# A gated cross-attention and expert kernel on one core: the first batch's front re-ordered on all five queues

## What is computed

```python
x = x + tanh(g_xattn) * attention(layernorm(x), ctx, Wq, Wk, Wv, Wo)
#   scores = (q k^T) * 0.125 ; softmax over the 1601 keys ; out = att v ; concat Wo
x = x + tanh(g_ffn) * experts(layernorm(x))
#   router softmax over 8, top 2 renormalised; each expert gelu(x w1 + b1) w2 + b2
```

## Time and profile before

| | us |
|---|---|
| runs shown | 1294.05, 1299.71, 1299.17; median 1299.17 |
| the profiled execution's own time | 1296.63 |
| its span in the profile | 1294.8 |
| TensorE busy | 1248.2 (96%) |
| VectorE busy | 1123.0 (87%) |
| ScalarE busy | 1085.2 (84%) |
| GpSimd busy | 553.5 (43%) |

### The profile page before, as it was taken

The page is one execution under the profiler, slowest core; times in us unless marked ns, Lnnn a source line. Parts: engine busy times, 40 slices in busy tenths (PEclk is TensorE's granted clock), DMA queues, the critical chain, the costliest instruction groups (busy, mean ns, idle before and its releaser), DMA issues.

```text
span 1294.8 us, 42224 instructions
## 1 busy us (share of the span) xinstructions
PE 1248.2 (96%) x16259; PEld 629.0 (49%) x16259; DVE 1123.0 (87%) x2012; ACT 1085.2 (84%) x2196; POOL 553.5 (43%) x1213
## 2 busy tenths in 40 slices
PE   7999999999999999999999999999999999999992
PEld 2344444444444444444444444444444444499992
DVE  7889999999999999999999999999999999356434
ACT  2788998999898989999999998999999898866661
POOL 6324344353536262726252635445353512146551
PEclk9999999999999999999999999999999999999996
DMA  3332222212121212131212121222211110388896
GB/s 95 90 91 65 66 78 60 68 55 73 50 77 47 79 48 80 43 87 37 82 42 71 54 69 60 65 66 60 69 55 42 51 43 6 98 254 245 264 272 229
DMA packets 61092, 112.94 MB, mean 87 GB/s; under 512 B 13052, under 2 KB 36476, under 8 KB 60748
## 3 DMA queue, kind: packets, MB, share of 16 engines
q1 hardware_dynamic: 54187, 97.98, 25.8%
q0 software_dynamic: 4320, 8.99, 2.0%
q10 hardware_dynamic: 2385, 3.27, 0.7%
HBM read 52.77 MB, written 13.71 MB: 51 GB/s over the span
## 4 chain that ended last, share of the span: by engine, by line
PE 75%; SPq 9%; POOL 7%; DMA 3%; issue 2%; DVE 2%; ACT 1%; ACTq 0%; POOLq 0%; DVEq 0%
PE pv L912 28%; PE st L821 16%; PE mxp L875 12%; SPq L416 7%; PE st L798 6%; PE st L1130 5%; PE mxp L1140 5%; POOL kf L659 2%; DVE mx L1679 2%; POOL ksp L664 2%; POOL rows L723 1%; POOL ksp L662 1%; DMA qpack<-mxT 1%; POOL ksp L656 1%; DMA arena<-results 1%
## 5 line engine op out<-in xcount | busy, mean ns | idle before, releaser
L1679 DVE TENSOR_REDUCE mx<-mxp 128x2 f32<-128x1024 f32 x768 | 916.3, 1217 | 42.6 <-PE mxp L875 35.2
L1169 ACT ACTIVATE arena<-st 128x512 f32<-128x512 f32 (+1 forms) x1664 | 883.8, 597 | 66.8 <-PE st L821 53.1
L912 PE MATMUL pv<-arena 128*32 128x256 f32 x6656 | 531.6, 391 | 0.6 <-ACT pv_sb L1176 0.3
L821 PE MATMUL st<-qpack,kpack 51*128 51x256 bf16 (+1 forms) x3328 | 486.2, 272 | 4.9 <-DMA qpack<-mxT 4.6
L875 PE MATMUL mxp<-kpack,qpack 48*128 48x512 bf16 x1502 | 406.3, 382 | 1.3 <-DVE mx L1679 1.3
L821 PEld LDWEIGHTS st<-qpack,kpack 51*128 51x128 bf16 (+1 forms) x3328 | 195.1, 95 | 279.0 <-ACT arena L1169 149.6
L912 PEld LDWEIGHTS pv<-arena 128*32 128x32 f32 x6656 | 131.2, 108 | 173.8 <-issue 104.4
L690 POOL CAST mxs<-nmx 128x8 bf16<-128x8 f32 x64 | 12.2, 191 | 344.9 <-DVE nmx L1689 344.7
L875 PEld LDWEIGHTS mxp<-kpack,qpack 48*128 48x128 bf16 x1502 | 123.0, 93 | 67.2 <-issue 38.8
L1332 ACT ACTIVATE arena<-st,bias 128x256 f32<-128x256 f32 (+1 forms) x172 | 74.9, 437 | 45.5 <-PE st L1130 42.0
L723 POOL DMA_INDIRECT rows<-xrow,pos x64 | 65.9, 1030 | 89.9 <-DVE pos L1534 75.1
(11 more groups left out here) (202 smaller groups left out, 990.1 us busy)
## 6 DMA issues: line engine op xcount, KB each, us to landing
kpack<-ksp SPq DMA_DIRECT2D x756, 50.0 KB
arena<-in_w12T SPq DMA_DIRECT2D x43, 576.0 KB, 4.8
arena<-in_ctxT SPq DMA_DIRECT2D x15, 800.5 KB, 4.6
qpack<-qsp SPq DMA_DIRECT2D x187, 32.0 KB
xblk<-rows SPq DMA_DIRECT2D x28, 132.0 KB, 4.2
rows<-in_pads SPq DMA_DIRECT2D x8, 264.0 KB
arena<-results SPq DMA_DIRECT2D x8, 256.0 KB, 6.8
arena<-results ACTq DMA_DIRECT2D x8, 256.0 KB, 7.4
```

Of the source, the lines that this page charges most:

```text
L821: ins = eng.matmul(ring[i][0:n, jj * N:(jj + 1) * N], kpack[rows, b % 2, g * JJ + jj, kt * P:kt * P + n], qpack[rows, b % 2, g * JJ + jj, ...
L912: ins = eng.matmul(pv[32 * j:32 * j + 32, 0:N], vaug[0:n, b % 2, kt, at:at + 32], pt[0:n, (2 * u + rg) % PT_BUFS, jj * N:(jj + 1) * N], st ...
L1169: eng.activation(pt[0:n, c % PT_BUFS, :], ring[bank_of["S", u, p]][0:n, :], ACT.Exp, scale=SCALE).then_inc(s_exp, 1)
L1679: eng.tensor_reduce(mx[:, tj, w, :], src[:, :, 0:WIN], AX.X, ALU.max).then_inc(s_red, 1)
```

## The change

In batch 0's front and loop:

- the first root: ScalarE takes a square root of the variance, VectorE its reciprocal and one Newton step in place of an integer guess and three. An exponential of a dummy value follows on ScalarE;
- TensorE turns the rows after one chunk of keys and makes the queries after two; window 0 comes ahead of the fourth chunk. ScalarE's copies follow the same order;
- 20 windows run ahead of unit 0 in place of 18. The first 15 are fp32 windows, the last five use packs;
- all four chunks of batch 0's values come in the front, behind windows 14, 16, 17 and 18 (before: one chunk behind window 5, three in units 1, 6 and 7);
- batch 1's values come at units 0, 3, 7 and 15 (before: 25, 26, 27, 30), its keys at 5, 9, 14 and 18 (before: 8, 9, 10, 17);
- SP issues batch 1's context load and the two ones DMAs at the start; the high key packs of groups 0 and 1 go ahead of the low ones;
- in every batch, GpSimd waits for the earlier packs ahead of its first write to `ksp`, and ScalarE waits only for GpSimd's splits.

```diff
-FIRST_K_AT = {8: 0, 9: 1, 10: 2, 17: 3}
+FIRST_K_AT = {5: 0, 9: 1, 14: 2, 18: 3}
-FIRST, LEAD = 18, 23
+FIRST, LEAD = 20, 23
-FIRST_WINDOWS_AT = ("0100201010210011010100000110111100010011000111211000",
+FIRST_WINDOWS_AT = ("0100101010100111000200000011020100011011011101021010",
...
-EARLY = FIRST
+EARLY = NMX + 2
-FIRST_V, FIRST_TURN = 5, 14
-FIRST_V_AT, FIRST_X_AT, FIRST_Q_AT = {1: 1, 6: 2, 7: 3}, 3, 5
+FRONT_V, FIRST_TURN = {14: 1, 16: 1, 17: 1, 18: 1}, 14
+FIRST_V_AT, FIRST_X_AT, FIRST_Q_AT = {0: 4, 3: 5, 7: 6, 15: 7}, 0, 4
+FIRST_NEWTON = 1
...
@@ SP
-            eng.dma_start(id_sb[:, :], ident).then_inc(s_id, 16)
+            eng.dma_start(x_sb[:, NT:2 * NT, :], xs[:, 1, :, :]).then_inc(s_x1, 16)
+            eng.dma_start(wv_sb[:, :], wv).then_inc(s_wv, 16)
+            eng.dma_start(ctx_sb[:, 1, :], ctxT[1]).then_inc(s_ctx[1], 16)
...
-            first_keys_high(eng, 0)
+            eng.wait_ge(s_kone, 1)
+            ones_rows(0)
+            first_keys_high(eng, 0, 0)
             first_query_rows(eng, range(PARTS), 0)
             first_query_rows(eng, range(PARTS - 1, PARTS), 1)
-            first_keys_low(eng, 0)
-            other_keys(eng, 1, 0)
-            eng.wait_ge(s_kone, 1)
-            ones_rows(0)
+            first_keys_high(eng, 1, 0)
+            first_keys_low(eng, 0, 0)
+            first_keys_low(eng, 1, 0)
             eng.wait_ge(s_mxT, 1)
             place_half(eng, 0, 0)
             for rg in range(RG):
                 other_keys(eng, 2, rg)
-            eng.dma_start(ctx_sb[:, 1, :], ctxT[1]).then_inc(s_ctx[1], 16)
             pack_keys(0, 3)
...
@@ GpSimd, split_keys
                     eng.wait_ge(s_khi, NK * b + c + 1)
+                    if c == 0:
+                        for g in range(NG):
+                            eng.wait_ge(s_kd[(b - 1) % 2][g], 16 * PACKS * ((b - 1) // 2 + 1))
...
@@ ScalarE, first_keys
-                    if c == 0:
-                        for g in range(NG):
-                            eng.wait_ge(s_kd[(b - 1) % 2][g], 16 * PACKS * ((b - 1) // 2 + 1))
-                        if b == 1:
-                            eng.wait_ge(s_mxp, RG * EARLY)
+                    eng.wait_ge(s_k3, NK * (b - 1) + c + 1)
+                    if b == 1 and c == 0:
+                        eng.wait_ge(s_mxp, RG * EARLY)
...
@@ ScalarE, front
+            eng.wait_ge(s_var0, 1)
+            eng.activation(tmp[:, :], var[:, :], ACT.Sqrt).then_inc(s_root0, 1)
+            eng.wait_ge(s_id, 16)
+            eng.activation(warm[:, :], id_sb[:, 0:1], ACT.Exp)
             first_keys(0, 0)
+            copy_rows(0)
+            first_keys(0, 1)
             first_high(0)
...
@@ VectorE, front
+            for n in range(3):
+                norm_step("X", 0, n)
+            eng.wait_ge(s_root0, 1)
+            eng.reciprocal(rstd[:, :], tmp[:, :]).then_inc(s_seed, 1)
+            for n in range(4 * FIRST_NEWTON + 1):
+                first_norm(n)
```

More of the change, by code:

```diff
@@ L138, in windows, with front_values @@
     return [divmod(n, NMX) for n in range(issued(u, p), min(to, GROUPS * NMX))]
+def front_values(n):
+    done = sum(FRONT_V[k] for k in FRONT_V if k < n)
+    return range(done, done + FRONT_V[n])
 def rank_at(b):
@@ L154, in prepared @@
         return "K", b + 1, keys_at(b)[r]
-    if b + 1 < B and r in V_AT:
+    if 0 < b < B - 1 and r in V_AT:
         return "V", b + 1, V_AT[r]
@@ L170, in take @@
         taken += 1
-    take("V", 0, 0)
-    take("M", 0)
+    for n in range(FIRST):
+        if n in FRONT_V:
+            for c in front_values(n):
+                take("V", *divmod(c, NV))
+        if n == FIRST_TURN:
+            take("M", 0)
     for u in range(B * UNITS):
@@ L184, in ring_banks @@
         if b == 0 and r in FIRST_V_AT:
-            take("V", 0, FIRST_V_AT[r])
+            take("V", *divmod(FIRST_V_AT[r], NV))
         if u in (FIRST_X_AT, FIRST_Q_AT):
@@ L436, in first_keys_low @@
                 if K_KIND[part] > 0:
-                    pack_key_rows(eng, 0, 0, part, rg)
+                    pack_key_rows(eng, 0, g, part, rg)
         def first_query_rows(eng, parts, rg):
@@ L833, in early_window @@
                 pair, rows = G * NMX + m, slice(rg * RSTEP, (rg + 1) * RSTEP)
[L834 to L838, removed]
+                if pair < 2 and rg == 0:
+                    eng.wait_ge(s_qearly, pair + 1)
+                if pair == NMX and rg == 0:
+                    eng.wait_ge(s_qlater, EARLY_HEADS - JJ)
                 if pair == 1 and rg == 0:
@@ L900, in weighted @@
                     eng.wait_ge(s_khi, NK)
-                if b == 0 and g == 0:
-                    eng.wait_ge(s_v, next(c for c, (t0, tn) in enumerate(VCH) if kt < t0 + tn) + 1)
-                elif r == 0:
+                if r == 0:
                     eng.wait_ge(s_v, NV * (b + 1))
@@ L1049, in _ @@
             eng.wait_ge(s_wk, 16)
-            for c in range(NK - 2):
-                keys(0, c)
+            keys(0, 0)
             eng.wait_ge(s_id, 16)
             turn_rows("X", 0)
-            keys(0, NK - 2)
+            keys(0, 1)
             eng.wait_ge(s_wq, 16)
             queries(0)
-            keys(0, NK - 1)
-            for n in range(issued(0, 0)):
+            keys(0, 2)
+            for n in range(FIRST):
                 maximum(*divmod(n, NMX))
-                if n == FIRST_V:
+                if n == 0:
+                    keys(0, 3)
                     eng.wait_ge(s_wv, 16)
-                    values(0, 0)
-                elif n == FIRST_TURN:
+                if n in FRONT_V:
+                    for c in front_values(n):
+                        values(*divmod(c, NV))
+                if n == FIRST_TURN:
                     turn_maxima(0)
@@ L1079, in _ @@
                         keys(b + 1, keys_at(b)[r])
-                    elif r in V_AT:
+                    elif b > 0 and r in V_AT:
                         values(b + 1, V_AT[r])
                 if b == 0 and r in FIRST_V_AT:
-                    values(0, FIRST_V_AT[r])
+                    values(*divmod(FIRST_V_AT[r], NV))
                 if u == FIRST_X_AT:
@@ L1377, in norm_step @@
                     own += NT
+                elif n == 2 and norm_no[kind, b] == 0:
+                    eng.wait_ge(s_dve, own)
+                    eng.tensor_scalar(var[:, :], stat[:, :, 1], LN_EPS, None, ALU.add
+                                      ).then_inc(s_var0, 1)
                 elif n == 2:
@@ L1746, in _ @@
             own += 2
-            for n in range(5):
-                norm_step("X", 1, n)
-            early_queries()
             eng.wait_ge(s_order, NE)
```

67 lines of the change are left out of this document (36 added, 31 removed).

## The result

| | before | after |
|---|---|---|
| median of 13 runs each on one chip, us | 1298.82 (1294.05 to 1302.70) | 1292.12 (1290.04 to 1297.51) |
| profiled execution, own time / span | 1296.63 / 1294.8 | 1291.35 / 1289.4 |

The ratio is 0.996, with a 95% interval of 0.9947 to 0.9973: 5.2 us (3.5 to 6.9) where 4.0 were forecast (the two medians lie 6.7 apart). The gain is clear of the noise. At 0.4% it is smaller than the 0.5% that I took as the bound of "no change", though the interval reaches just past that bound.

A forecast was written before the change was run, and what follows sets the result against it. Up to unit 26 SP's list of issues was taken as the bound, behind it TensorE's work; 1.2 us from the list plus 2.8 behind unit 26 gave 4.0, so 1292.6 us profiled or 1295.2 against the median; range 1290.0 to 1300.0.

The forecast's parts named there:

- one of my own signs of being wrong: Listed signs of a wrong forecast, up to unit 53 and the end; one was SP waiting for a split.
- Window 0 and the start of SP's list: Batch 0's front: window 0 takes 11.3 us, not 12.30; SP's list starts 0.2 us earlier, at about 32.35.
- How long the list is: SP's issues up to group 2's maxima: 0.5 less for the context load, 0.35 for half the first pack's extra 0.7.
- SP comes to the packs at 68.9: Ahead of group 2's maxima: batch 1's last split ends near 67.3, before SP reaches the six packs at 68.9.
- TensorE reaches unit 26 at about 73, and waits 2 to 3 us: Ahead of unit 26: TensorE is early and waits for SP's placing; unit 26 starts at 75.5.
- Together 2.8 us of TensorE: Behind unit 26: TensorE saves 2.05 us of values and 0.75 for two windows fewer.
- VectorE would allow more: Behind unit 26: VectorE reduces two windows fewer (2.4 us) and starts on the first with unit 26.
- The steady part: Every batch: GpSimd instead of ScalarE waits for packs; costed at nothing.
- The faster queue: Rival, chance 0.16: up to 3.8 us of SP's slow issues go, unit 26 at 73; gain 6.5, so 1292.7 us.
- The eaten gain: Rival, chance 0.20: packs landing late, or values that only filled time VectorE would hold TensorE, leave about 1 us: 1298.2.
- The slower one: Rival, chance 0.07: batch 1's last split comes late, SP stands at the six packs; 3.2 us slower, 1302.4.
- The rule against the change: Front, table load behind the root: the skill's 2.66 us per switch would cut window 0's gain to 0.6, the sum to 3.6.

The follow-up runs named there:

- the controls: The kernel before and the changed kernel, each run and profiled again unchanged on another chip; 1308.07 us (one run) and 1304.80 us.
- c_after: The changed kernel run and profiled again, unchanged, on another chip; 1304.80 us, ratio 0.9948 to the kernel before.
- e6_turn_first: The changed kernel with batch 0's first chunk of values behind the turn of group 0's maxima, not ahead of it; 1302.81 us in one run.
- c_before: The kernel before, run and profiled again unchanged on another chip; 1308.07 us in one run.
- e3_values_back: The changed kernel with batch 1's four chunks of values back at units 25, 26, 27 and 30; 1306.33 us, ratio 0.9969 to the kernel before.
- e1_root_alone: The kernel before with only batch 0's new root (square root on ScalarE, reciprocal, one Newton step); 1308.82 us in one run.
- e2_old_root: The changed kernel with the old root (integer guess, three Newton steps, no square root on ScalarE); 1307.41 us in one run.

## Why the prediction was right, and where its steps failed

**The sum was right: 4.0 forecast, 3.5 to 6.9 measured,** and unit 53's keys came 4.83 us earlier (3.65 in the controls, 4.2 in the mean). Of this, 2.36 lie behind unit 26 and 2.5 or 1.3 ahead of it, where I had put 2.8 and 1.2. Several steps beneath the sum were wrong, and one of my own signs of being wrong came: SP waited for a split. Behind unit 26 the mechanism was right and its size a little high. Ahead of it the 1.2 was near by luck: I had it from SP's list, but the chain there left SP, and what bounds unit 26 now is the way of TensorE and VectorE from 31 us on.

- **Window 0 and the start of SP's list** ("about 32.35", 0.2 earlier): it was at 31.09. The root was as priced or better (`xn` at 5.64 for 5.95) and the 1.0 us for the values is confirmed, but I took the third chunk at 1.56, and this price isn't a chunk's, it is that of the time at which it ran. With two profiles on each side the gain is 0.5, and counted from the first matmul 0.3. Neither arrives at unit 26 as such (`c_after`, `e6_turn_first`).
- **"How long the list is"** (0.5 + 0.35): from start to group 2's maxima it took 40.54 for 41.54, so 1.0 shorter, but with 1.3 and 0.5 of standing in it. The issues themselves shrank by 2.8: the load's 0.5, 1.1 in the 24 packs (15.64 for 16.74) and 1.2 in the query packs (7.92 for 9.12). Half of the queue's extra of 0.7 was too little, and for the 24 packs the reason is the ones: late in the new order they cost 2.9 us of issues. For the query packs it isn't, since they take 7.92 with the ones late too; why they got shorter is open, and they vary (8.39 in `c_before`, 8.90 in `e3_values_back`). I had read one slow row, 1.35, where their effect lies over the whole list and on the landing of group 0's maxima.
- **"SP comes to the packs at 68.9", the split at 67.3, 1.6 us of cover:** the split came at 67.61, as forecast within 0.3, and SP would have been there at 67.1. The cover was -0.5. This step failed on SP's side: what SP gained turned the last split into the bound.
- **"TensorE reaches unit 26 at about 73, and waits 2 to 3 us":** it waited 0.42. Its work from unit 0 on was as large as I said, and ScalarE's stall went, but 1.42 us of waits for VectorE's windows came in its place, where before had 0.24; I had counted none. SP, the split and TensorE now arrive within 0.5 us of one another, which is why three edits to the front and the list moved little.
- **"Together 2.8 us of TensorE":** the mechanism holds, with 2.36. Its sum was 0.4 too large. Which term was, depends on the order in which they are taken out: 2.01 for the values and 0.35 for the windows, or 1.54 and 0.82, where I had 2.05 and 0.75. Their busy times overlap and don't add up. What I gave in half a sentence, that "VectorE would allow more", is a condition and not a remark: with two windows more behind unit 26 VectorE does not allow it, and the values alone give 0 to 0.45.
- **The steady part, costed at nothing:** nothing in the list of unit 26, perhaps 0.5 to 1.0 over 15 batches. That it was a condition of the new order I missed: 4.6 us without it.

**The rivals.** The faster queue: largely true of the queue (2.3 us on the key and query packs), while the two loads behind the ones took 2.67 and 1.97 us as before, as its counter-argument had it. It brought little, because unit 26 "at TensorE's own pace" is 73.84 and not 73. The eaten gain: its second reason, values that fill time in which VectorE would hold TensorE, is what the old order with early values showed; two windows less took that reason away. The slower one: its mechanism is the bound now, with 0.5 us, and not the 5.6 that a loss would take.

**The rule against the change.** The second table load takes 1.28 us at 4.56, and the exponential follows at 5.85, at once; ScalarE then waits 0.83 us for TensorE. The 2.66 us with a drain of the Trainium skill (ScalarE: Activation LUTs, What ACT_TABLE_LOAD costs) don't show here. By an estimate with that page's figure the load would have ended at 4.56 + 2.66 = 7.22, 0.34 behind the 6.88 at which the first copy began.

## To carry to other kernels

Where one queue is the bound, write down for each of its waits how far the next thing behind it is: here the split and TensorE lay within half a microsecond of SP's list once it was shorter, and of the 2.8 us taken from its issues SP gave 1.8 back by standing for others. Where two engines are nearly full in one stretch (values on TensorE, windows on VectorE), taking work from one gives only what the other has left, so their work is to be moved together. Compare by landmarks and with a second profile of both kernels when microseconds matter: a start that moves by 1 us and a dip of the clock that moves up to 3 look like effects of an edit.

## What I had not expected of the hardware

- The same eight matmuls of a chunk take 1.56 or 0.84 us in the first 13 us of the program, at a granted clock of 1.00 in both; the change from one to the other fell anywhere from about 8 us (`e1_root_alone`) to over 12 (`e2_old_root`, whose first window at 12.21 still took 1.86 where others have 1.13), and in one and the same kernel before or after the third chunk.
- Two DMAs of ones stretch the issues behind them: 2.9 us over 25 issues in the kernel with the ones late. Behind the later pair a load of rows takes 2.66 and a context load 1.97, where a context load elsewhere took 0.44; that this is the ones' doing too was not tested. The context load sent 11 us later took 0.36 to issue, but the six packs took 1.24 more.
- Behind waits of TensorE of 1.83, 2.33 and 2.92 us the granted clock fell to 0.50 to 0.74 for some 4 us, down to the lower of its two levels (1.2 of 2.4 GHz). Behind waits of 1.81, 1.63, 1.59 and 1.46 us it did not.
